# The sum of the second residual: by a DMA that adds into SBUF instead of by GpSimd's additions

## What is computed

```
x1  = x  + softmax(norm(x) M_b + c_b, masked) V_b      # M_b, c_b, V_b: small, from ctx and the weights
h   = gelu(norm(x1) (alpha1 sign(w1))^T + b1)          # 256 -> 1024, exact gelu
out = x1 + h (alpha2 sign(w2))^T + b2                  # 1024 -> 256
```

## Time and profile before

| | us |
|---|---|
| median of 3 runs (332.15 to 333.83) | 333.26 |
| the profiled execution | 331.71 |
| its span, first to last instruction | 329.9 |

### The profile page before, as it was taken

How to read it: one execution, slowest core, us unless ns; L and a number is a source line. 1 busy time by engine, 2 the same in 40 slices (tenths; PEclk the granted TensorE clock), 3 DMA queues, 4 the chain that set the end, 5 groups by cost and what they waited for, 6 DMA issues and landing times.

```text
span 329.9 us, 6163 instructions
## 1 busy us (share of the span) xinstructions
PE 297.6 (90%) x2055; PEld 201.5 (61%) x2055; DVE 285.9 (87%) x637; ACT 261.3 (79%) x330; POOL 247.9 (75%) x412
## 2 busy tenths in 40 slices
PE   1999999598989898989899989898989899999994
PEld 1735666265657575757576657575666666676673
DVE  0999996999999999999998999999999796976444
ACT  1079553799898989898989798989899989788770
POOL 2480608695999999999999999999999857668331
PEclk9995755999999999999999999999999999999998
DMA  7957668283547493839474747473535425251311
GB/s 238 329 203 156 75 104 112 63 171 64 127 66 201 69 194 69 195 74 193 80 193 80 193 80 194 80 192 71 138 66 143 67 79 67 78 130 30 100 64 64
DMA packets 85183, 40.33 MB, mean 122 GB/s; under 512 B 77464, under 2 KB 80672, under 8 KB 85152
## 3 DMA queue, kind: packets, MB, share of 16 engines
q1 hardware_dynamic: 84240, 39.90, 53.6%
q10 hardware_dynamic: 912, 0.05, 0.2%
HBM read 12.80 MB, written 8.39 MB: 64 GB/s over the span
## 4 chain that ended last, share of the span: by engine, by line
PE 40%; POOL 28%; DVE 13%; DMA 8%; issue 6%; ACT 5%; SPq 0%; POOLq 0%; DVEq 0%; ACTq 0%
PE psY L1336 17%; PE psZ L1351 16%; POOL xh L458 8%; DMA xT_lo<-w_sb 6%; POOL x1b L482 4%; POOL w_sb L493 4%; POOL rstd L447 4%; POOL sc L469 3%; PE psY L1239 3%; DVE st_raw L717 3%; PE psW L1312 2%; DMA x_in<-in_x 2%; POOL vare L442 2%; PE psW L1292 2%; ACT psY L579 1%
## 5 line engine op out<-in xcount | busy, mean ns | idle before, releaser
L1351 PE MATMUL psZ<-sgn2T,h_hi 128*128 128x256 f16 x512 | 115.2, 273 | 0.0
L1351 PE MATMUL psZ<-sgn2T,h_lo 128*128 128x256 f16 x512 | 115.2, 273 | 0.0
L1336 PE MATMUL psY<-xT_hi,sgn1T 128*128 128x512 f16 x256 | 97.0, 379 | 15.3 <-DMA xT_lo<-w_sb 12.2
L579 ACT ACTIVATE psY<-psY,b_col,alpha1x 128x512 f32<-128x512 f32 x128 | 93.5, 750 | 12.4 <-PE psY L1336 9.6
L839 DVE SCALAR_TENSOR_TENSOR h_lo<-psY,h_scale,h_hi 128x1024 f16<-128x1024 f32 x64 | 81.2, 1269 | 18.8 <-ACT h_hi L588 18.8
L1336 PE MATMUL psY<-xT_lo,sgn1T 128*128 128x512 f16 x256 | 97.0, 379 | 0.0
L588 ACT ACTIVATE h_hi<-psY,h_scale 128x1024 f16<-128x1024 f32 x64 | 71.2, 1113 | 4.5
L493 POOL TENSOR_TENSOR w_sb<-w_sb,x1b 128x256 f32<-128x256 f32 x62 | 47.1, 791 | 14.3 <-DVE w_sb L853 14.3
L1351 PEld LDWEIGHTS psZ<-sgn2T,h_hi 128*128 128x128 f16 x512 | 50.1, 98 | 9.7 <-DVE h_lo L839 0.2
L1351 PEld LDWEIGHTS psZ<-sgn2T,h_lo 128*128 128x128 f16 x512 | 50.1, 98 | 9.5
L1336 PEld LDWEIGHTS psY<-xT_hi,sgn1T 128*128 128x128 f16 x256 | 25.0, 98 | 43.1 <-issue 16.1
(11 more groups left out here) (145 smaller groups left out, 449.3 us busy)
## 6 DMA issues: line engine op xcount, KB each, us to landing
out_x<-w_sb SPq DMA_DIRECT2D x15, 512.0 KB, 3.1
x_in<-in_x SPq DMA_DIRECT2D x6, 512.0 KB, 4.2
ctx_sb<-in_x SPq DMA_DIRECT2D x6, 512.0 KB, 4.2
w_sb<-in_L_ffn_w SPq DMA_DIRECT2D x2, 1024.0 KB, 8.2
wkq<-in_x SPq DMA_DIRECT2D x4, 512.0 KB, 4.1
ctx_sb<-in_ctx SPq DMA_DIRECT2D x1, 1024.0 KB, 6.0
out_x<-w_sb SPq DMA_DIRECT2D x2, 256.0 KB, 2.1
wkq<-in_L_xattn_Wk SPq DMA_DIRECT2D x1, 256.0 KB, 7.2
```

What stands on the lines that cost most here:

```text
L579: nc.scalar.activation(y, y, ACT.Gelu, bias=b1_col[:, c:c + 1], scale=alpha1x[:, c:c + 1]).then_inc(gelu_done, 1)
L1336: last = nc.tensor.matmul(psY[q % 2][:, c % 2, :], sgn1T[:, c, k, :], part[b % 2][:, :, k, :], start=(n == 0), stop=(n == 2 * KD - 1))
L1351: last = nc.tensor.matmul(Z[n][:, (j % 2) * D:(j % 2 + 1) * D].rearrange("p (k t) -> p k t", k=KD), part[q][:, u, j * P:(j + 1) * P], sgn2 ...
```

## The change

`add_residual` of batches 0 to 14 is one DMA instead of four additions. GpSimd issues it, with x1b as source and z_sb as destination and the addition as its accumulate operation; it reads both tiles and writes the sum to z_sb. Two new semaphores, one for each buffer, count its landing. `store(b)` and `add_b2(b+2)`, which waited for out_ready, wait for these. Batch 15 is as before; out_ready is now counted up by it alone.

```diff
@@ -252,6 +252,7 @@
         z_added = sem("z_added")
         z_scaled = sem("z_scaled")
         x1b_ready = sem("x1b_ready")
+        z_summed = [sem(f"z_summed{n}") for n in range(2)]
         out_ready = sem("out_ready")
         out_half_ready = sem("out_half_ready")
 
@@ -347,11 +348,11 @@
                     return
                 if b == B - 1:
                     for n in range(2):
-                        sp.wait_ge((out_ready, out_half_ready)[n], (B, 1)[n])
+                        sp.wait_ge((out_ready, out_half_ready)[n], 1)
                         sp.dma_start(out_v[b, :, 2 * n:2 * n + 2, :], z_sb[b % 2][:, 2 * n:2 * n + 2, :]) \
                           .then_inc(out_stored[b % 2], 16)
                     return
-                sp.wait_ge(out_ready, val(b, 1, 1))
+                sp.wait_ge(z_summed[b % 2], dma_val(b))
                 sp.dma_start(out_v[b, :, :, :], z_sb[b % 2]).then_inc(out_stored[b % 2], 16)
 
             def load_w(dst, src, name):
@@ -477,7 +478,7 @@
                     pool.wait_ge(loaded["b2"], 16)
                 pool.wait_ge(x1_ready, val(b, 2, 2))
 
-                wait(pool, out_ready, val(b - 2, 1, 1))
+                wait(pool, z_summed[b % 2], dma_val(b - 2))
                 for j in range(T):
                     last = nc.gpsimd.tensor_tensor(x1b[b % 2][:, j, :], x1[b % 2][:, j, :], b2_bc[:, :],
                                                    ALU.add)
@@ -489,7 +490,11 @@
                     return
                 pool.wait_ge(x1b_ready, val(b, 1, 1))
                 pool.wait_ge(z_scaled, val(b, 2, 1 if b == B - 1 else 2))
-                for j in range(2 if b == B - 1 else T):
+                if b < B - 1:
+                    nc.gpsimd.dma_start(z_sb[b % 2], x1b[b % 2][:, :, :], accum_op=ALU.add) \
+                        .then_inc(z_summed[b % 2], 16)
+                    return
+                for j in range(2):
                     last = nc.gpsimd.tensor_tensor(z_sb[b % 2][:, j, :], z_sb[b % 2][:, j, :],
                                                    x1b[b % 2][:, j, :], ALU.add)
                 last.then_inc(out_ready, 1)
```

## The result

| | before | after |
|---|---|---|
| median | 332.76 us (4 runs, 332.15 to 333.83) | 346.76 us (4 runs, 345.88 to 348.04) |
| profiled execution, span | 331.71 us, 329.9 us | 347.6 us, 345.8 us |

The change makes the kernel slower: ratio 1.041, interval 1.037 to 1.045, 14.0 us between the medians. The forecast was 333.4 (no change) in a range of 331.0 to 353.0. The range holds the time, the likeliest case does not. The time came out at the rival "the transposes land late" (345). In the later rounds of runs, on other chips, the kernel before took 334.6 to 335.0 us in the median, about 2 us more than here, so of the 14.0 us some 2 may belong to the round and not to the change.

What follows compares the result with a forecast made beforehand. A 16.91 us loop through VectorE, GpSimd's norm and ScalarE was taken as the bound, the additions off it. Steady state 0 and tail -0.66 + 0.8 = +0.1 us on 333.26 gave 333.4 us, range 331.0 to 353.0.

Steps and rivals of the forecast that it cites:

- the transposes land late: Rival: xT_lo lands 1.9 us later, 1.2 beyond the slack, on 10 full steps: +12 us, 345; chance 0.17.
- the likeliest case: The sum's landing is covered by GpSimd's slack, no change: 333.4 us, own range 331.7 to 334.9; chance 0.42.
- The loop of 16.91 us: Stats, GpSimd's norm, ScalarE's rounding and h_hi, VectorE back to stats: said to set the step; the additions are off it.
- slack of 1.75 us: GpSimd's long norm and shift instructions read as hidden waits for VectorE, about 0.85 + 0.9 us in each step.
- GpSimd was the bound: Rival: the loop is misread and VectorE becomes the next bound, steps of 15.95 us: 323, half of it 328; faster 0.09.
- Removal of the additions: Frees VectorE's split by up to 0.64 us a step, worth 0 in steady state, 0 to 0.66 us in the tail.
- Issue, D: GpSimd's time to issue the DMA: 1.2 us, between 0.57 and 2.78, hidden by GpSimd's slack.
- The wait at add_b2, L: From GpSimd's turn at the DMA to the sum's landing: 7.4 us, free up to 8.3, bounds 3.1 to 13.8.
- the doubled store: Way of pricing L: 1.2 us of issue plus twice the 3.1 us median of a plain 512 KB store, 7.4 us.
- The traffic: DMA beside the batch's two transposes: xT_lo 0.8 us later against TensorE's 0.7 us slack, about nothing per step.
- The tail: At the end of the kernel: -0.66 us for the freed split, +0.8 for contention, +0.1 us in all.
- SyncE's store: Store now waits for the sum, with turn_lo and the load of x behind it; add_b2 feels a late landing long before.

Runs made afterwards that it cites:

- adds_raw: adds_first with VectorE's raw_statistics(b+2,1) moved ahead of lo(b,3): 327.57 us, ratio 0.981 to the kernel before.
- no_sum: The changed kernel with neither DMA nor additions for batches 0 to 14 (out is z alone there): 337.32 us, ratio 1.009 to the kernel before.
- adds_first: late_both with add_b2(b) moved right behind norm(b,1), ahead of norm(b+4,0): 334.33 us, ratio 0.997 to the kernel before.
- best: adds_raw with the DMA for batches 0 to 9 only, GpSimd's additions from batch 10 on: 336.48 us, ratio 1.006 to the kernel before.
- three_x1b: The changed kernel with a third x1b buffer, so add_b2 waits for the sum of one batch earlier: 345.8 us, ratio 1.032 to the kernel before.
- late_both: Changed kernel with three x1b buffers, DMA behind add_b2, store one step later; batches 12 to 14's DMA also waits for the low half's transposes: 337.06 us.
- plain_copy: The changed kernel with the DMA copying x1b to z_sb without adding, same bytes, place and waits: 336.86 us, ratio 1.006 to the kernel before.
- dma_to_9: The changed kernel with the adding DMA for batches 0 to 9 only, GpSimd's additions from batch 10 on: 336.66 us, ratio 1.003 to the kernel before.

## Where the prediction was right and where it was wrong, point by point

The time lies in the stated range, but near a rival that I had given 0.17, and the likeliest case, no change at 0.42, is 13 us away. That the rival's 345 comes within 2 us of the measured 346.76 is luck: its mechanism, late transposes, is the one that the runs showed, but its sum puts the cost into steps that hardly pay any and has no clock in it.

- **What bounds the kernel.** Half right. The loop of 16.91 us through VectorE and ScalarE exists, but I took GpSimd's long durations (1.05 and 1.52 us) for slack of 1.75 us. They were none: with VectorE's gap closed and the additions kept, the step stays at 16.98 us. Even the 0.27 us that I had added to the loop between the stats (200.96) and the norm (201.23) was GpSimd still at its shift, which ends at 199.62 + 1.52 = 201.14. GpSimd was a limit of the same length, so its relief alone shows nothing, and neither does VectorE's. The rival "GpSimd was the bound" (323 to 328) named a gain that needed a second edit: 327.57 in adds_raw. Its steps of 16.4 us are not the 15.95 of that rival.
- **Removal of the additions.** Forecast 0; measured +0.24 us a step (no_sum), because the neighbour moved. I had asked what the split gains (it did gain: 1.21 us) and not what the next two-input operation, add_b2, would come to lie on. adds_first shows it: steps of 16.95 us with the additions gone. The rule of the Trainium skill (SBUF — State Buffer, Who interferes with whom) that I had read beside rows 2 and 4, that a VectorE instruction with two SBUF inputs and a GpSimd one that reads SBUF hold each other up, was the right one, and I applied it to one pair of instructions only. The trace of best agrees: 4.94 us for the split beside additions that stand back to back, more than the length of any one of them.
- **Issue, D.** Forecast 1.2 us; 0.89 measured. Right within its bounds and without effect. That VectorE's operations at 188 to 190.5 read PSUM or are tiny was not quite so: the statistics from 187.53 on are four instructions of 0.35 us that read x in SBUF. Nothing hung on it.
- **The wait at add_b2, L.** Forecast 7.4 us of the 8.3 allowed; in step 8 it is 6.0. Right for the steady part; in the tail, with no norm of a later batch in between, add_b2 waits up to 6.3 us. three_x1b takes all of it away and wins 1 to 3 us. The Trainium skill's figures gave an estimate of 4.4 us (DMA: Bandwidth & Descriptors, Anatomy of one DMA; Collectives: The Full Stack, The bandwidth ceiling); the measured median from issue to landing is 5.8 us, and 5.0 in late_both, where it meets a transpose of the attention half instead of the FFN's, so the estimate was low and the doubled store nearer.
- **The traffic, the step that failed.** "About nothing per step" held only where there is slack. I priced it on one transpose, xT_lo landing 0.8 us later, with a plain copy as the measure. It landed 1.0 later (4.1 for 3.1), so that term was about right, but two others were left out: the high half's transpose lands 2.3 us later (5.4), and SyncE's queue takes 0.8 us more to issue each of them. TensorE's waits for xT_lo grew from 12.2 to 18.2 us. A plain copy is also no measure for an adding one: in plain_copy the same bytes cost nothing.
- **The tail, the largest error.** I took the steady slack of 0.7 us and a single 0.8 us for the end. The DMA costs the tail 10.4 us over 5 batches: TensorE has no slack there (it waits 1.09 us once more, then 0.80, then not again), so each late transpose counts in full: 5.95 us more of waiting. Behind two of these waits TensorE's clock fell to 0.50, some 3.4 us more, a term that no part of the forecast has. In the steady part the changed kernel loses 1.2 us to the DMA (3.66 less no_sum's 2.47), by one fall of the clock, and dma_to_9 nothing. The rival put its +12 us on the ten full steps; late_both and dma_to_9 put the cost in the tail.
- **SyncE's store.** Priced at nothing; no run tested it by itself.

What stays open: why an adding DMA holds up a transpose more than a plain one, beyond its double time on the DMA engines; the last 1 us of the tail's 10.4; and why TensorE's clock fell behind some of its waits and not behind others.

## What to carry to other kernels

Before work is taken off an engine, ask which neighbour slides into its place and what it will share SBUF with there; moving that neighbour was worth as much as the removal cost. Price a new DMA on every transfer that it overlaps and on the queue that issues them, and ask of each who waits for it: here about 2 us of delay cost the kernel 10 us on the FFN half's transposes of five batches and nothing on those of the attention half. Price the tail by itself, because there the slack of the steady state does not exist, and read the granted clock wherever TensorE has waited. When a removal and a reorder each show nothing, try them together: two limits of equal length hide each other.

## What the runs showed of the hardware

- A DMA that adds 512 KB from SBUF into SBUF took 5.0 to 5.8 us from issue to landing (medians) and 3.04 us of all 16 DMA engines, with a transpose beside it in every run; the plain copy of the same bytes in the place of the 5.8 took 3.4 and 1.47.
- The FFN half's transposes beside the adding DMA land in 5.4 and 4.1 us instead of 3.1, and their issue on SyncE's queue takes a median of 2.05 us instead of 1.23; beside the plain copy they land in 3.9 and 3.1. The attention's high half beside the adding DMA lands in 4.6 to 5.3 us instead of 3.1.
- The issue of the adding DMA takes GpSimd 0.87 to 0.93 us (medians; single ones 0.83 to 1.06), that of the plain copy 0.65.
- A two-input VectorE instruction on SBUF beside GpSimd's two-input additions back to back can be held up by several of them: 4.94 us for work of 1.2, once, in best.
- TensorE's granted clock was 0.50 (1.2 GHz) for some 3 us in three places of the changed kernel's execution, each behind a wait of 2.02 to 2.92 us, and the same product then took 0.63 us instead of 0.38.
